# Convolutional attention on one core: values in four column quarters, row sums from key tiles added on GpSimd

## What is computed

```python
x = x + _L0_conv_ref(_gn(x), ...)      # group norm over 4 channels
# inside, per image:
q = jnp.einsum('bchw,oc->bohw', x, qW)              # 256 x 1024
q = q.reshape(B, NUM_HEADS, -1, KEY_DIM)            # 8192 queries of 32 numbers
k = _bn(_dw_conv(x, kdwW, 2), ...)                  # 3 x 3, stride 2
k = jnp.einsum('bchw,oc->bohw', k, kW)              # 32 keys' numbers x 256 places
v = jnp.einsum('bchw,oc->bohw', _bn(_dw_conv(x, vdwW, 2), ...), vW)
attn = jax.nn.softmax(jnp.einsum('bnqd,bdl->bnql', q, k) / HEAD_DIM ** 0.5, axis=-1)
ctx = jnp.einsum('bnql,bld->bnqd', attn, v)
out = jnp.einsum('bchw,oc->bohw', ctx.reshape(B, 256, px, px), oW)
```

## Time and profile before

| | |
|---|---|
| median of 3 runs | 2161.94 us (2161.93 to 2164.02) |
| the profiled execution | 2174.15 us, its span 2172.4 us |
| conv attention | to about 842 us of the span |
| TensorE busy in the whole span | 90% |

### The profile page before, as it was taken

The page is one execution under the profiler, slowest core; times in us unless marked ns, Lnnn a source line. Parts: engine busy times, 40 slices in busy tenths (PEclk is TensorE's granted clock), DMA queues, the critical chain, the costliest instruction groups (busy, mean ns, idle before and its releaser), DMA issues. The chain is left out here.

```text
span 2172.4 us, 44335 instructions
## 1 busy us (share of the span) xinstructions
PE 1961.4 (90%) x11636; PEld 1466.1 (67%) x11636; DVE 1375.0 (63%) x3923; ACT 989.7 (46%) x2194; POOL 1029.3 (47%) x1367
## 2 busy tenths in 40 slices
PE   3999999999999998888898888887189999999997
PEld 2666666666666654665666666555189999999997
DVE  3676766767767665787788878876434444444443
ACT  0554555555455554444344333342045555555554
POOL 1221121212112111445554555555658888888887
PEclk9999999999999999999999999998589999999999
DMA  5322222222223222111111111111234444454454
GB/s 195 74 66 71 61 71 64 65 70 65 70 60 73 62 61 74 54 36 38 41 38 41 36 38 35 42 38 40 66 57 64 64 65 63 63 65 65 63 65 51
DMA packets 175423, 131.90 MB, mean 61 GB/s; under 512 B 33437, under 2 KB 164933, under 8 KB 175301
## 3 DMA queue, kind: packets, MB, share of 16 engines
q0 software_dynamic: 55808, 52.50, 15.1%
q1 hardware_dynamic: 118341, 77.16, 13.6%
q10 hardware_dynamic: 1152, 0.54, 0.1%
HBM read 31.47 MB, written 46.71 MB: 36 GB/s over the span
## 5 line engine op out<-in xcount | busy, mean ns | idle before, releaser
L1664 POOL DMA_INDIRECT out<-f_y,f_rows x272 | 424.1, 1559 | 45.5 <-POOL f_waited L1662 41.7
L447 DVE TENSOR_REDUCE neg_max<-s_bank 128x2 f32<-128x512 f32 x512 | 329.5, 685 | 133.5 <-PE s_bank L715 131.4
L1727 DVE SCALAR_TENSOR_TENSOR f_hidden<-f_silu,f_rows,f_h_bank 128x341 f32<-128x341 f32 x272 | 155.4, 571 | 307.6 <-ACT f_silu L1696 279.7
L567 ACT ACTIVATE probsT<-st_bank 128x512 f32<-128x512 f32 x512 | 276.6, 593 | 133.9 <-PE st_bank L733 133.6
L1096 POOL DMA_INDIRECT routed<-a_rows,a_target_idx x256 | 253.2, 989 | 68.6 <-issue 68.3
L335 POOL TENSOR_TENSOR waited<-nothing 128x1 int32<-128x1 int32 x64 | 12.1, 189 | 514.0 <-DVE q_low L436 514.0
L1473 PE MATMUL a_score_bank<-t_eT,t_gT 128*128 128x512 f32 x512 | 252.4, 617 | 1.2 <-DVE a_val L1140 1.2
L745 PE MATMUL o_bank<-probsT,v_ones 128*64 128x512 f32 x1024 | 248.0, 605 | 0.0
L1775 PE MATMUL f_y_bank<-w,f_hiddenT 114*128 (+1 forms) x1632 | 230.8, 277 | 1.3 <-ACT f_hiddenT L1688 1.3
L715 PEld LDWEIGHTS s_bank<-k_stack,q_stack 96*128 96x128 f32 x1024 | 141.9, 193 | 113.4 <-issue 94.0
L733 PE MATMUL st_bank<-q_stack,k_stack 98*128 98x512 f32 x512 | 214.0, 484 | 0.6 <-ACT probsT L567 0.5
(11 more groups left out here) (210 smaller groups left out, 3591.7 us busy)
## 6 DMA issues: line engine op xcount, KB each, us to landing
q_stack<-q_high SPq DMA_DIRECT2D x512, 64.0 KB, 2.3
f_rows<-routed SPq DMA_DIRECT2D x272, 66.0 KB
q_stack<-q_low POOLq DMA_DIRECT2D x256, 64.0 KB, 2.6
out<-X SPq DMA_DIRECT2D x16, 512.0 KB, 3.2
X<-in_x SPq DMA_DIRECT2D x1, 6144.0 KB, 22.1
out<-f_y,f_rows POOLq DMA_INDIRECT x272
q_stack<-max_rows SPq DMA_DIRECT2D x256, 4.0 KB
routed<-a_rows,a_target_idx POOLq DMA_INDIRECT x256
```

The costliest lines, as they stand in the source:

```text
L447: dve.tensor_reduce(neg_max[:, i % 2, CT * j:CT * (j + 1)], s_bank[h % 2][:], AX_X, ALU.max, negate=True).then_inc(max_ready, 1)
L567: act.activation(probsT[:, i % 2, c, lt, :], st_bank[lt][:], ACT.Exp).then_inc(exp_done, 1)
L1664: pool.indirect_dma_start(out=out, out_offset=bass.IndirectOffsetOnAxis(ap=rows[:, i, TOKEN:TOKEN + 1].bitcast(I32), axis=0), in_=y[:, i, ...
```

## The change

- Two pairs form an octet. `values` runs in even iterations, for the octet of the two iterations before: each of the four chunks fills 32 partitions of `o_bank`, with 32 weight columns and no column of ones. `probsT` has four slots instead of two.
- Row sums: GpSimd adds the two key tiles of each chunk (`add_keys`), and `row_sums` in odd iterations multiplies the four results with 32 weight columns of which only column o is one. All four octets of an image gather in `sum_bank`. The image's sums are copied once, turned once (`turn_sums`, i = 2) and inverted once (`invert_sums`).
- `turn_context` runs in odd iterations as their last work. ScalarE copies the turned context to `raw` (`evacuate_turned`); VectorE multiplies half an image at a time (`scale`, i = 3 and 5). `project` and `add_output` move to i = 5 and 7, and 6 and 7, of the next period.
- The maxima are turned into `c_bank`, block 0, since `sum_bank` takes the bank of `m_bank`; new waits keep the two uses apart.
- `keys_values` writes two halves of 64 columns, five taps and four; VectorE adds them.
- Queries stand ahead of values. Their split buffers have two slots instead of four.
- On VectorE the channel statistics are dealt out over i = 2 and 4, group norm moves to the end of i = 0.

```diff
+                def add_keys(b, i):
+                    if i % 2 == 0:
+                        wait(pool, sums_full, octet_no(b, i // 2) - 1)
+                    for c in range(CHUNKS_PER_PAIR):
+                        pool.wait_ge(exp_done, PAIR_EXPS * pair_no(b, i) + LT * (c + 1))
+                        pool.tensor_tensor(key_sum(i // 2, CHUNKS_PER_PAIR * (i % 2) + c), probsT[:, i % 4, c, 0, :],
+                                           probsT[:, i % 4, c, 1, :], ALU.add).then_inc(key_sums, 1)
...
+                def scale(b, k):
+                    dve.wait_ge(c_out, OCTETS * (b + 1))
+                    wait(dve, out_full, 2 * (b - 1) + k + 1)
+                    part = slice(ROWS * k, ROWS * (k + 1))
+                    dve.tensor_tensor(context[:, part, :], raw[:, part, :],
+                                      rsum[:, part].unsqueeze(2).to_broadcast([P, ROWS, KD]), ALU.mult
+                                      ).then_inc(scaled, 1)
...
                 def exps(b, i, c):
                     if c == 0:
-                        wait(act, o_full, pair_no(b, i) - 1)
+                        wait(act, o_full, octet_no(b, i // 2) - 1)
+                        wait(act, key_sums, CHUNKS_PER_PAIR * (pair_no(b, i) - 3))
...
+                def evacuate_turned(b, slot, o):
+                    act.wait_ge(c_full, octet_no(b, o) + 1)
+                    wait(act, scaled, 2 * b - (o < OCTETS // 2))
...
-                    for n, t in enumerate((4, 0, 1, 2, 3, 5, 6, 7, 8)):
+                    halves = ((4, 0, 1, 2, 7), (5, 3, 6, 8))
+                    for n in range(len(halves[0])):
+                        for part, taps in enumerate(halves):
...
                     elif k == 2:
                         pe.wait_ge(q_low_done, Q_CHUNKS * b + 2)
+                        wait(pe, out_done, 2 * (b - 2) + 1)
...
+                def values(b, slot, o):
+                    if o == 0:
                         pe.wait_ge(v_in, 16 * LT * (b + 1))
-                    pe.wait_ge(exp_done, PAIR_EXPS * (pair_no(b, i) + 1))
-                    wait(pe, ctxT_full, pair_no(b, i))
+                    pe.wait_ge(exp_done, PAIR_EXPS * 2 * (octet_no(b, o) + 1))
+                    wait(pe, ctxT_full, octet_no(b, o))
                     for lt in range(LT):
-                        for c in range(CHUNKS_PER_PAIR):
-                            last = pe.matmul(o_bank[HALF * c:HALF * (c + 1), :], v_ones[:, slot, lt, :],
-                                             probsT[:, i % 2, c, lt, :], start=(lt == 0), stop=(lt == LT - 1))
+                        for cc in range(OCTET_CHUNKS):
+                            i, c = divmod(cc, CHUNKS_PER_PAIR)
+                            last = pe.matmul(o_bank[QUAD * cc:QUAD * (cc + 1), :], v_rows[:, slot, lt, :],
+                                             probsT[:, (2 * o + i) % 4, c, lt, :], start=(lt == 0), stop=(lt == LT - 1))
...
+                def row_sums(b, o):
+                    if o == 0:
+                        wait(pe, sums_out, b)
+                    pe.wait_ge(key_sums, OCTET_CHUNKS * (octet_no(b, o) + 1))
+                    for cc in range(OCTET_CHUNKS):
+                        last = pe.matmul(sum_bank[QUAD * cc:QUAD * (cc + 1), :], ones_at[:, o, :], key_sum(o, cc),
+                                         start=(o == 0), stop=(o == OCTETS - 1), skip_group_check=True)
```

299 lines of the change are left out of this document (178 added, 121 removed).

## The result

| | before | after |
|---|---|---|
| median | 2161.94 us (5 runs, 2156.71 to 2165.76) | 2139.0 us (5 runs, 2135.87 to 2144.19) |
| ratio | | 0.9894, 95% interval 0.9872 to 0.9916 |
| the profiled execution | 2174.15 us, span 2172.4 | 2136.72 us, span 2135.0 |
| beat of a middle image | 49.1 to 49.2 us | 46.7 to 46.9 us, once 50.0 |
| the second stage's first matmul | 842.84 us | 814.83 us |

A forecast was written before the change was run, and what follows sets the result against it. TensorE's instruction order was taken to bound the conv-attention stage. Per image -6.75 us of work plus waits of 3.4, 0.45 and 0.3 made -2.6; 15.5 images gave -40, ends +3: 2161.94 to 2125 us, range 2080 to 2172.

The forecast's parts named there:

- Values, row sums, taps, turning, statistics: TensorE terms per image: values -7.5 us, row sums +4.0, taps -1.5, turning context and sums -1.05, statistics wait -0.7.
- the lower bound: Value block of four column quarters: 1.87 us if all run at once, against 3.7 us if two at once.
- ScalarE, +3.4: Second shifted scores wait for exponentials behind ScalarE's copies: 0.64 us per even, 0.4 per odd iteration, net +3.4 us per image.
- Queries and projection, 0: TensorE's query and projection blocks: the sum had no term for them, so no change per image.
- The output add, +0.45: VectorE in i = 6: the add ends late behind two row maxima and delays the queries, +0.45 us per image.
- the scaling, +0.3: VectorE in i = 3: the scaling stands ahead of two row maxima in a short iteration, +0.3 us per image.
- GpSimd: Sixteen key adds of 128x512 per image at 1.27 us each, 20.3 us more per image, forecast as hidden.
- Rival 3: GpSimd's adds hold up VectorE's scalings, mainly in i = 3: +2.9 us per image, 2170 us; chance 0.12.
- Queries ahead of values, "hidden": Queries moved ahead of values: forecast to cost nothing, their DMAs starting 1.9 us earlier on SyncE's queue.
- Ends of the stage, +3: First stage's ends: first taps save some 2 us, longer chain after the last values adds 5 us, together +3 us.
- -6.0 us per image: Fast end of the forecast's range: no more ScalarE waits than today, stated as 2075 us.
- its bound of 4.2: Upper bound of ScalarE's added wait per image; the range's slow end, all waits at upper bounds without rival 3, was 2158 us.

The follow-up runs named there:

- the run by quarters: Changed kernel with the eight matmuls of a value block ordered quarter by quarter instead of key tile by key tile: 2143.6 us (one run).
- the run with the moved blocks: Changed kernel with values and row sums between the turning of the maxima and the second shifted scores, not at the iteration's end: 2131.26 us, ratio 0.9852.
- the run with the late copy: Changed kernel with ScalarE's copy of o_bank moved into the next, odd iteration, behind the high part of the maxima: 2135.61 us, ratio 0.9891.

## Why the prediction was right in sign and 14 us too low

- **Values, row sums, taps, turning, statistics**: right within 0.3 us each (table). Quarters do run together; the lower bound was the right one to take. The Trainium skill (TensorE: Matmul & The Clock Gate, Part 3) has 2.38 times for three column tiles; here four give a block of twice the records in 1.86 us in place of the 1.87 of two, so against two there is no loss in this shape. The same section says that matmuls keep strict order in start and end; the run by quarters does not fit that.
- **ScalarE, +3.4**: mis-sized, +2.55, 0.3 of which is the wait for VectorE in i = 3. The step that failed took today's 0.63 us as "nothing holds it" and put all waiting on the copies. What holds is the pace of two banks, 2.01 us; the copies add 0.24 and 0.09, 1.3 us per image. The sum was still right because of what I had at nothing, and that is luck:
- **Queries and projection, 0**: +2.2, or some +1.1 without what comes back in the first shifted scores. A value block behind the queries, and transpositions behind the projection, start late. The Trainium skill (TensorEngine Tiling (Array Packing), Key Properties) says that a change of tiling mode drains TensorE. The 0.10 us of a change of columns agrees with it; the 0.18 us that transpositions of full width show as well do not come from such a change, and their cause stays open.
- **The output add, +0.45, and the scaling, +0.3**: 0.56 for the add (the run that moves it). The scaling's term has the wrong place: it does stand ahead of two maxima, but in i = 4, behind it, the stretch to the second shifted scores is longer than in the other even iterations by under 0.1 us. The wait in i = 3 (+0.3 and +0.5) comes from the inversion of the sums and the statistics ahead of the maxima, for which the sum had nothing.
- **GpSimd**: the adds take 1.25 to 1.30 us alone (forecast 1.27) and are hidden in all images but one. Rival 3's mechanism was real, and in the changed kernel its price came due once, 3.2 us, about half of it the clock behind the wait (an estimate, half of 3.4 us). That it came due only once is luck of the order, as the ten images of 47.8 to 48.2 us in the run with the moved blocks show. The Trainium skill (SBUF — State Buffer, SBUF: two separate sides) describes it, whole instruction against whole instruction; the 1.20, 3.03 and 3.65 us of one scaling agree.
- **Queries ahead of values, "hidden"**: undone, it costs 8.5 us per image with all that follows from it, which I had not worked out: I followed its DMAs, not what stands on VectorE's queue behind `query_low`.
- **Ends of the stage, +3**: start -3.2 (forecast -2), tail +5.3 (+5). The last image was 1.9 us longer, where the sum had half an image's gain, -1.3.
- **From 40 to 23**: the forecast had 15.5 images at -2.6 and ends of +3, -37. The stage ended 28.0 us earlier: 9 us less: the odd image 3.2, the last image 3.2, 0.3 us per image on images 1 to 14 another 4.3, less a net 1.5 at the start, in image 0 and in the tail. The remaining 5 us between 28.0 and the medians' 22.9 can't be placed: the rest of the program is the same code and took between 1318 and 1326 us in the profiles of the changed kernel and the ten variants on chips like its own (1320.1 in its own, 1329.6 in that of before, which was 12 us over its median).
- **The prediction's own figures**: two ends of the forecast's range do not follow from its terms. -6.0 us per image gives 2072, not 2075, and ScalarE at its bound of 4.2 with the other waits as stated gives 2137, not 2158.

## What to carry to other kernels

Count a stretch that runs between two handovers against its own shortest time (here two banks and two exponentials, 2.0 us), before blaming what stands in a queue; and put independent blocks inside it, not at the end of the iteration. When TensorE's order changes, follow for every engine what stands behind the one operation that the moved block feeds or delays: the queue behind `query_low` cost, with what followed from it, more than any term of the sum. Between VectorE with two SBUF inputs and GpSimd, fix the order with a wait: in i = 3 of the changed kernel the first add ended 0.03 us ahead of the scaling, and one pause undid that. And price a wait of TensorE with the clock that can follow it: ten of the eleven waits of about 1.3 us in the run with the moved blocks were followed by 3.4 us at half the clock, which cost more than the wait.

## What the hardware showed unasked

- GpSimd's queue paused for 1.44 us ahead of its 129th and its 245th DMA issue of this stage, in the kernel before (420.6 and 776.3 us), in the changed one (396.1 and 737.4) and in all twelve variants (1.44 to 1.47 us, once 1.56). Taking out the 256 adds did not move it to another issue. Before, nothing waited for it.
- When VectorE's scaling waits for an add and GpSimd has a second add ready, the second add may go first as well (3.03 us in i = 5 of the changed kernel), or not (1.83 us in the run with the late copy). The second add's distance from the scaling's start doesn't decide it: it waited at 0.75 us there, and went first at 0.67 and, in image 0, at 0.78 in the changed kernel.
- A subtraction of 128x1 took 2.03 to 2.05 us beside the adds, 0.16 without: the length of an operation says nothing about its exposure.
